# Two heads' scores in row halves of the array, one exponential over two banks, and a new order of work

## What is computed

```
x = x + L0_attn_ref(layernorm(x), ...)   # one head of width 64, causal softmax
x = x + L0_ffn_ref(layernorm(x), ...)    # one product in fp8
x = x + L1_attn_ref(layernorm(x), ...)   # 16 heads of width 16, rotary, causal softmax
x = x + L1_ffn_ref(layernorm(x), ...)    # sigmoid(r) * (relu(k)^2 @ W_v)
...
scores = jnp.einsum('bhsd,bhtd->bhst', Q, K) / jnp.sqrt(jnp.float32(D_K))
scores = jnp.where(causal[None, None], scores, -jnp.inf)
attn = jax.nn.softmax(scores, axis=-1)
out = jnp.einsum('bhst,bhtd->bhsd', attn, V)
```

## Time and profile before

| | |
|---|---|
| runs | 3010.06 us median of 3 (3002.6 to 3011.0) |
| the profiled execution | 3001.34 us, its span 2999.5 us |
| PE busy | 2646.3 us, 88% |
| DVE busy | 2010.0 us, 67% |
| ACT busy | 1566.6 us, 52% |
| POOL busy | 392.3 us, 13% |
| mean granted clock of PE | 0.946 of 2.4 GHz |

### The profile page before, as it was taken

The page is one execution under the profiler, slowest core; times in us unless marked ns, Lnnn a source line. Parts: engine busy times, 40 slices in busy tenths (PEclk is TensorE's granted clock), DMA queues, the critical chain, the costliest instruction groups (busy, mean ns, idle before and its releaser), DMA issues.

```text
span 2999.5 us, 49751 instructions
## 1 busy us (share of the span) xinstructions
PE 2646.3 (88%) x17886; PEld 1164.8 (39%) x18098; DVE 2010.0 (67%) x4386; ACT 1566.6 (52%) x3137; POOL 392.3 (13%) x418
## 2 busy tenths in 40 slices
PE   3677879999899898989989898998989989999995
PEld 2343423433343343434334343443434334433344
DVE  4445577776776767777665777777567577777832
ACT  1223336565555545565554555656454565666761
POOL 2212201010201111020100202020110100000011
PEclk8788879999999999999999999999999999999997
DMA  2333113030311313030120313122131121111101
GB/s 53 90 98 84 34 57 104 18 105 15 89 53 35 96 43 93 29 107 22 49 85 29 86 47 95 35 65 69 30 98 34 34 85 56 44 46 35 31 24 37
DMA packets 239478, 175.56 MB, mean 59 GB/s; under 512 B 89793, under 2 KB 238978, under 8 KB 239234
## 3 DMA queue, kind: packets, MB, share of 16 engines
q1 hardware_dynamic: 237376, 170.52, 20.1%
q10 hardware_dynamic: 1858, 1.84, 0.2%
HBM read 87.30 MB, written 84.41 MB: 57 GB/s over the span
## 4 chain that ended last, share of the span: by engine, by line
PE 69%; DVE 10%; ACT 6%; SPq 5%; issue 4%; DMA 3%; DVEq 1%; POOL 1%; another core or an unknown queue 1%; POOLq 0%; ACTq 0%
PE psum L1480 15%; PE psum L1466 14%; PE psum L1441 9%; DVE mx L1208 6%; SPq L719 4%; PE psum L1377 4%; PE psum L1409 4%; ACT probs L1010 3%; PE psum L1299 3%; DMA rest_dram<-parts 2%; PE psum L1508 2%; PE psum L1351 2%; PE psum L1527 2%; PE psum L1515 2%; PE psum L1428 2%
## 5 line engine op out<-in xcount | busy, mean ns | idle before, releaser
L1208 DVE TENSOR_REDUCE mx<-psum 128x1 f32<-128x512 f32 (+3 forms) x2560 | 1389.2, 600 | 409.1 <-PE psum L1447 229.2
L1010 ACT ACTIVATE probs<-psum 128x512 f32<-128x512 f32 (+3 forms) x2560 | 1186.7, 542 | 639.6 <-PE psum L1466 282.3
L1466 PE MATMUL psum<-qst,kst 98*128 98x512 bf16 (+7 forms) x2348 | 670.6, 357 | 84.5 <-ACT probs L1010 48.6
L1480 PE MATMUL psum<-probs,vs 128*17 128x512 f32 (+3 forms) x5120 | 600.0, 541 | 1.8 <-ACT probs L1010 0.4
L1441 PE MATMUL psum<-kst,qst 64*128 64x512 bf16 (+3 forms) x2560 | 450.9, 364 | 83.7 <-ACT probs L1010 33.8
L1466 PEld LDWEIGHTS psum<-qst,kst 98*128 98x128 bf16 (+1 forms) x2560 | 226.9, 99 | 505.0 <-ACT probs L1010 200.6
L1441 PEld LDWEIGHTS psum<-kst,qst 64*128 64x128 bf16 x2560 | 124.1, 94 | 541.3 <-DVE mx L1208 190.5
L1469 PE MATMUL psum<-maskf,identb 128*128 128x128 bf16 x1024 | 208.2, 225 | 4.1 <-issue 2.8
L856 POOL TENSOR_SCALAR vare<-mv 128x4 f32<-128x4 f32 x64 | 14.6, 228 | 1384.2 <-DVE mv L1106 1384.2
L970 ACT ACTIVATE probs<-psum 128x1024 f32<-128x1024 f32 x80 | 74.5, 938 | 150.0 <-PE psum L1357 100.7
L1447 PE MATMUL psum<-maskq,identh 64*128 64x128 bf16 x2048 | 151.3, 224 | 0.0
(11 more groups left out here) (133 smaller groups left out, 2548.8 us busy)
## 6 DMA issues: line engine op xcount, KB each, us to landing
main_dram<-parts SPq DMA_DIRECT2D x256, 128.0 KB
rest_dram<-parts SPq DMA_DIRECT2D x128, 128.0 KB
qst<-main_dram SPq DMA_DIRECT2D x128, 128.0 KB, 2.7
kst<-main_dram SPq DMA_DIRECT2D x128, 128.0 KB, 2.7
v_dram<-vst SPq DMA_DIRECT2D x64, 136.0 KB, 4.5
vs<-v_dram SPq DMA_DIRECT2D x64, 136.0 KB, 2.3
xs<-x_in SPq DMA_DIRECT2D x16, 512.0 KB, 4.0
x_dram<-xs SPq DMA_DIRECT2D x16, 512.0 KB, 2.9
```

Source lines behind the costliest of these rows:

```text
L1010: act.activation(probs[:, HG * (step_no(b, hg, k) % 2) + h, 0:cols], home("scores", item)[:, 0:cols], ACT.Exp, scale=DK1 ** -0.5).then_inc ...
L1208: dve.tensor_reduce(mx1[:, n % 2, 2 * g + odd, i % TPC, c:c + 1], bank(PLAN.home["max", item[:5]][odd], 0, width(i, c)), AX.X, ALU.max).th ...
L1466: ins = pe.matmul(ps[:, 0:CH - off], kst[rows, kslot, odd, g, P * (kb % TPC):P * (kb % TPC + 1)], qst[rows, qslot, odd, g, off:CH], start= ...
L1480: ins = pe.matmul(bank(7, off, CH, rows=VW, row=32 * h), vtile[:, h, :], probs[:, HG * (step_no(b, hg, k) % 2) + h, 0:CH - off], start=(kb ...
```

## The change

**Scores.** A `scores` job is now a pair of heads. The stacks `kst` and `qst` are laid out so that each head of the pair has its own 64 partitions: part 0 holds its MAIN rows (64), part 1 its REST rows and the two rows of the maximum (34 rows). The job is four matmuls, two side by side for each part, and four small ones for the mask. It takes an aligned pair of banks, one bank per head, and counts as R. `maskf` is gone.

**Exponential.** One instruction reads both banks, 2 x 512, where two instructions read 512 each. FAR_S goes from 4 heads to 2 pairs.

**Start.** The three memsets of `kst` and `qst` on DVE are gone; POOL sets the part-1 half of `kst` to ones, behind its first `root` job.

**Order.** The planner now assumes 0.31 us for leaving F and 0.1 or 0.14 us for the other switches (0.1 us for any before), STICK is 100 instead of 10, LEAD 85 instead of 66, and V0's assumed duration 1.85 instead of 0.9. The `max` jobs' banks are still E.

```
-LEAD = 66.0
+LEAD = 85.0
...
-STICK = 10.0
+SWITCH = {("F", "R"): 0.31, ("F", "C"): 0.31, ("R", "F"): 0.1, ("R", "C"): 0.1, ("C", "F"): 0.14, ("C", "R"): 0.14}
+STICK = 100.0
...
-FAR_M, FAR_S = 2, 4
+FAR_M, FAR_S = 2, 2
...
-                    time += 0.1
+                    time += SWITCH.get((mode, md), 0.0)
...
-    add("PE", "V0", c, key(), 0.9, *both(0), lat=0.1, claim="P", mode="F")
+    add("PE", "V0", c, key(), 1.85, *both(0), lat=0.1, claim="P", mode="F")
...
-                add("PE", "scores", (b, hg, k, h), key + h / 2, 0.215 * size + (0.055 if diagonal else 0),
-                    ("rows", me), ("load k", (b, hg, kb // TPC)), ("exp", far), lat=0.1, claim="P", mode="F")
-                add("ACT", "exp", (b, hg, k, h), key + h / 2, 0.05 + 0.427 * size, ("scores", (b, hg, k, h)),
+                add("PE", "scores", (b, hg, k, pair), key + pair, 0.43 * size + (0.11 if diagonal else 0),
+                    ("rows", me), ("load k", (b, hg, kb // TPC)), ("exp", far), lat=0.1, claim="D", mode="R")
+                add("ACT", "exp", (b, hg, k, pair), key + pair, 0.07 + 0.853 * size, ("scores", (b, hg, k, pair)),
...
+                    if item == (0, 0, 0):
+                        pool.memset(kst[:, :, 1, :, :], 1.0).then_inc(done, 1)
...
-                    act.activation(probs[:, HG * (step_no(b, hg, k) % 2) + h, 0:cols], home("scores", item)[:, 0:cols],
-                                   ACT.Exp, scale=DK1 ** -0.5).then_inc(S["exp"], 1)
+                    at = HG * (step_no(b, hg, k) % 2) + 2 * pair
+                    act.activation(probs[:, at:at + 2, 0:cols], two_banks("scores", item)[:, :, 0:cols], ACT.Exp,
+                                   scale=DK1 ** -0.5).then_inc(S["exp"], 1)
...
-            dve.memset(kst[HALF + REST:P, :, 0, :, :], 1.0).then_inc(S["stacks"], 1)
-            dve.memset(kst[REST:HALF, :, 1, :, :], 1.0).then_inc(S["stacks"], 1)
-            dve.memset(qst[REST:HALF, :, 1, :, :], 0.0).then_inc(S["stacks"], 1)
...
-                    g, odd = divmod(h, 2)
-                    rows = slice(0, P if odd else HALF + RROWS)
...
-                    ins = pe.matmul(ps[:, 0:CH - off], kst[rows, kslot, odd, g, P * (kb % TPC):P * (kb % TPC + 1)],
-                                    qst[rows, qslot, odd, g, off:CH], start=True, stop=not diagonal)
+                    for part in range(2):
+                        for odd in range(2):
+                            rows = slice(HALF * odd, HALF * odd + (HALF if part == 0 else RROWS))
+                            ins = pe.matmul(two[odd][:, 0:CH - off], kst[rows, kslot, part, pair, keys],
+                                            qst[rows, qslot, part, pair, off:CH],
+                                            start=(part == 0), stop=(part == 1 and not diagonal))
...
```

More of the change, by code:

```diff
@@ L343, in head_jobs @@
         add("SP", "load k", me, pos - LEAD - 25, 0.4, ("put", (b, q, 2 + hg // 2)),
-            *[("scores", n and (*n, h)) for h in range(HG)], lat=4.5)
+            *[("scores", n and (*n, pair)) for pair in range(HG // 2)], lat=4.5)
         slot = block_before(b, hg, q, QRING)
@@ L377, in head_jobs @@
             two = step_before(b, hg, k, 2)
[L378 to L379 removed]
+            for pair in range(HG // 2):
+                scored.append((b, hg, k, pair))
                 far = scored[-1 - FAR_S] if len(scored) > FAR_S else None
[L381 to L385 removed]
+                add("PE", "scores", (b, hg, k, pair), key + pair, 0.43 * size + (0.11 if diagonal else 0),
+                    ("rows", me), ("load k", (b, hg, kb // TPC)), ("exp", far), lat=0.1, claim="D", mode="R")
+                add("ACT", "exp", (b, hg, k, pair), key + pair, 0.07 + 0.853 * size, ("scores", (b, hg, k, pair)),
+                    ("values", two), lat=0.1, free=("scores", (b, hg, k, pair)))
+            add("PE", "values", (b, hg, k), key + 5, 0.84 * size, ("exp", (b, hg, k, 0)), ("exp", (b, hg, k, 1)),
                 ("load v", (b, hg, kb // TPC)), ("values", (b, hg, k - 1) if kb else None), lat=0.1, claim="V" if kb == 0 else None, mode="C")
@@ L483, in freed @@
     if kind == "max":
-        return "max d", (*item, PLAN.home[name].index(n))
+        return FREED_BY[kind], (*item, PLAN.home[name].index(n))
     if kind == "WO0":
@@ L610, in build @@
         v_dram = nc.dram_tensor("v_dram", [B, NHG, P, NT, HG * VW], F32, kind="Internal").ap()
-        names = KINDS + ["weights", "weights later", "const", "stacks", "ready", "ready later", "chain d", "chain p", "apart"]
+        names = KINDS + ["weights", "weights later", "const", "ready", "ready later", "chain d", "chain p", "apart"]
         names += [f"load x {i}" for i in range(2)] + [f"store x2 {i}" for i in range(2)]
@@ L742, in _ @@
                     if old:
-                        for h in range(HG):
-                            wt.job("scores", (*old[:2], k, h))
+                        wt.job("scores", (*old[:2], k, 0))
+                        wt.job("scores", (*old[:2], k, 1))
                     loaded = S[f"{kind} {slot}"]
@@ L828, in _ @@
                                base=0, pattern=[[-1, P]], channel_multiplier=1).then_inc(done, 1)
[L829 to L831 removed]
+            n += 1
             wt.wait_ge("const", n)
@@ L1005, in _ @@
                 elif kind == "exp":
-                    b, hg, k, h = item
+                    b, hg, k, pair = item
                     wt.job("values", step_before(b, hg, k, 2))
@@ L1440, in _ @@
                         rows = slice(HALF * odd, HALF * (odd + 1))
-                        ins = pe.matmul(two[odd][:, 0:cols], qst[rows, qslot, odd, g, P * (i % TPC):P * (i % TPC + 1)],
-                                        kst[rows, kslot, odd, g, 0:cols], start=True, stop=c < q)
+                        ins = pe.matmul(two[odd][:, 0:cols], qst[rows, qslot, 0, g, P * (i % TPC):P * (i % TPC + 1)],
+                                        kst[rows, kslot, 0, g, 0:cols], start=True, stop=c < q)
                     if c == q:
@@ L1461, in _ @@
                     off = span(q, kb)
-                    ps = home(kind, item)
-                    g, odd = divmod(h, 2)
-                    rows = slice(0, P if odd else HALF + RROWS)
+                    two = [bank(n) for n in PLAN.home[kind, item]]
+                    keys = slice(P * (kb % TPC), P * (kb % TPC + 1))
                     diagonal = kb >= TPC * q
-                    ins = pe.matmul(ps[:, 0:CH - off], kst[rows, kslot, odd, g, P * (kb % TPC):P * (kb % TPC + 1)],
-                                    qst[rows, qslot, odd, g, off:CH], start=True, stop=not diagonal)
-                    if diagonal:
-                        ins = pe.matmul(ps[:, 0:P], identb[:, :], maskf[:, :], start=False, stop=True)
+                    for part in range(2):
[4 more added lines that the diff above has]
+                                            start=(part == 0), stop=(part == 1 and not diagonal))
+                    if diagonal:
+                        for part in range(2):
+                            for odd in range(2):
+                                rows = slice(HALF * odd, HALF * (odd + 1))
+                                ins = pe.matmul(two[odd][:, 0:P], identh[rows, part, :], maskk[rows, part, :],
+                                                start=False, stop=(part == 1))
                     ins.then_inc(S["scores"], 1)
@@ L1473, in _ @@
                     q, kb = STEPS[k]
-                    for h in range(HG):
-                        wt.job("exp", (b, hg, k, h))
+                    wt.job("exp", (b, hg, k, 0))
+                    wt.job("exp", (b, hg, k, 1))
                     v_loaded(wt, b, hg, kb // TPC)
```

28 lines of the change are left out of this document (9 added, 19 removed).

## The result

| | before | after |
|---|---|---|
| median of the runs | 3008.60 us (3002.6 to 3011.0, 4 runs) | 3109.69 us (3103.1 to 3111.4, 4 runs) |
| ratio | | 1.0335, 95% interval 1.0312 to 1.0358 |
| span of the profiled run, granted clock | 2999.5 us, 0.946 | 3109.4 us, 0.953 |

The change costs 3.4%, or 101 us. The forecast was 3062: right in direction, inside its range of 2960 to 3130, and 48 us short. After is where the forecast's own range (3019 to 3110) and that of the rival that puts every wait on top (3110 to 3150) meet.

A forecast was written before the change was run, and what follows sets the result against it. PE was taken to bound the kernel, with 508 us of its span lost to waits and lower clock. 2999.5 - 75.5 - 5 + 120 + 21 = 3060, with 1.8 us around the span 3062 us; range 2960 to 3130.

The forecast's parts named there:

- Scores in halves: PE's scores: two slots of two matmuls side by side take 0.44 us a pair as before; price 0, 13 us either way.
- Changes of use: PE switching between kinds of matmul: 2594 fall to 1799, at 0.095 us each, 75.5 us less.
- that way of being wrong: Sign against the forecast: a change out of F in fact costs 0.31 us, giving 132 us more gain.
- One exponential per pair: ACT: the double form takes 1.02 us, four single ones 2.06, so ACT's work changes by 0 us.
- Banks: Scores wait on PE for banks held by the double exponential: +120 us in light steps, +21 in other blocks.
- the count's 201.9: Us of waits counted in PE's new order, at 377 places where scores reuse the home of the scores just before.
- The sign of 3.1 us for a light step: Steps in blocks with PE work under 3.0 us a step would take near 3.1 us if the forecast was right.
- Start: Without DVE's three memsets the first layernorm and all behind it come 5.1 us earlier: -5 us; POOL's fill costs 0.
- Waits in lost time: Faster rival: bank waits on PE replace time lost anyway, 2919 us at best, 2995 at most, middle 2965; chance 0.22.
- cancelling: Rival: 78 to 95 us of new waits on PE cancel the gains, within 0.3% of no change; chance 0.08.
- The clock: Rival: short waits bring PE's light steps to a granted clock of 0.88, +110 us, so 3170; chance 0.07.
- Everything on top: Slower rival: the whole 202 us of bank waits on PE is new, and more, 3110 to 3150 us; chance 0.13.

The follow-up runs named there:

- e5: After with any two banks for a pair of scores, an exponential per head, and before's LEAD, STICK and switch prices: 3010.9 us, 1.0019 of before.
- e11: Before with only STICK raised from 10 to 100: 3110.45 us, 1.0343 of before.
- e3: After planned with the old numbers (LEAD 66, STICK 10, 0.1 us per change of use, V0 0.9): 3137.19 us, 1.0426 of before.
- e6: As e5, but the two heads of scores take neighbouring banks in three aligned homes, each still with its own exponential: 3159.6 us, 1.0515 of before.
- e2: After with max pairs planned on an aligned pair of banks instead of any two: 3122.04 us, 1.0372 of before.
- e9: After with double exponential kept, scores in any two neighbouring banks (six places instead of three), before's LEAD, STICK and switch prices: 3106.5 us, 1.0324 of before.
- e12: e5 with LEAD 58 instead of 66, STICK 20 instead of 10, and the early fill of e8: 3031.36 us, 1.0083 of before.
- e4: Before, with single heads, planned with the new numbers (LEAD 85, STICK 100, dearer changes of use, V0 1.85): 3113.79 us, 1.0348 of before.
- e7: After in the same order, each exponential reading only the left half of its two banks' columns, probabilities zeroed first: 3047.41 us, 1.0135 of before.
- e10: e5 with STICK 15 instead of 10, scores up to three places ahead instead of two, and the early fill of e8: 3027.73 us, 1.0060 of before.
- e1: After with separate banks: scores pairs only in homes 0-1 and 2-3, max pairs in any two of banks 4 to 6: 3240.13 us, 1.0768 of before.
- e8: After with GpSimd's fill of the key tiles' second half issued right behind the constants: 3098.71 us in one run.

## Why the prediction was right or wrong

**The terms.** Three of them can be measured in the two traces; the waits are then what is left of the 110 us by which the span grew. The time at half clock is read from the records of the granted clock: 324 us before and 294 after, in which PE is busy for 196 and 212 us. Half of that, 98 and 106, is my estimate of what the lower clock cost.

| term | forecast | measured |
|---|---|---|
| changes of use, 2594 to 1799 | -75.5 | -75.5 (0.09 to 0.11 each between neighbouring starts, in every direction) |
| start | -5 | -1.3 |
| time at the lower clock | 0 | 98 to 106, +8 (less by up to 5, as before lacks records of matmuls) |
| waits of PE, with the rest (halves, keys) | +120 +21, 0 +-25 | +179, by difference |
| sum | +60.5 | +110 |

**Scores in halves: right.** A pair takes 0.44 (1442.91 to 1443.35 above), and e5, which has them, is within 0.3% of before.

**Changes of use: right.** For example `values` to `max` 0.99 (1441.70 to 1442.69), `max` to scores 0.22 without a change. The 0.31 of the planner is the price of a change in no distance, so that way of being wrong did not occur. But the term stood alone in my sum, and the numbers that bring it have a price of their own: e11 saves 37 us of changes and is 100 us slower.

**One exponential per pair: right on the path, with a size off.** ACT by form in after:

```profile
L1009 ACT ACTIVATE probs<-psum 128x1024 f32<-128x1024 f32 x896 | 898.0, 1023 | 621.0 <-PE psum L1464 513.1 <-PE psum L1471 90.6 <-PE psum L1483 17.1
```

1023 ns as read from the first layer. ACT's busy time fell from 1566.6 to 1505.8 us, not by 0; how much of it the span saw is open (e3 is 0.9% below e6, with another V0 and another order).

**Banks: right mechanism, and this is the term that was mis-sized.** "let the new wait swallow half of the 0.2 of short ones" and "of the 43 us in the other blocks I take half" took 61 us off the count's 201.9. The traces show about 20 off: 179 us by the table came on top, 38 more than the 141 that I took. In the light steps 0.36 us was new where the forecast had 0.32, 135 us in all against 120; the other 44, where it had 21, came outside them. With 4 us less at the start and up to 8 from the clock, that is the gap of 49 us between the spans. (The sign of 3.1 us for a light step did not follow from the forecast's own terms: 2.42 + 0.49 + 0.32 = 3.23, and 3.27 was measured.)

That the count came so near is partly luck, though. It looked only at scores behind the scores just before them. It missed three things: scores wait in ScalarE's queue (the second pair's exponential follows the first's), a bank may be held by an older job, and maxima wait for VectorE in the same way. Within one form it ranked e2 and e3 correctly; between forms it failed: by its waits alone it said 42 us for e6 over e5 (149 measured) and 97 for e9 under e3 (31). Mended for these after e5 to e11, as told in the expectation of e12, it gives, in us above before:

| | after | e2 | e3 | e4 | e5 | e6 | e7 | e9 | e10 | e11 | e12 | e1 |
|---|---|---|---|---|---|---|---|---|---|---|---|---|
| waits counted, less before's 135 | 197 | 189 | 198 | 142 | 98 | 207 | 136 | 131 | 119 | 112 | 79 | 114 |
| changes of use x 0.095 | -76 | -69 | -63 | -45 | -61 | -62 | -76 | -63 | -72 | -37 | -64 | -53 |
| sum | 121 | 120 | 135 | 97 | 37 | 146 | 61 | 68 | 47 | 75 | 14 | 61 |
| measured | 101 | 112 | 128 | 104 | 7 | 156 | 43 | 96 | 18 | 100 | 23 | 230 |

Eleven of twelve are within 30 us. Of the 197 us of after, it puts 119 on scores behind exponentials (54 to 173) and 70 on maxima behind VectorE (44 to 114). PE's own idle time in the traces has 69 and 50 us more of the two (above). The 5 us of the early fill in e10 and e12 are not in the table. e1 it misses by 169 us. The larger part of that is the clock, which the count does not have: e1 is at half clock for 713 us, and PE is busy for 431 of them where before it is for 196; half of the difference is 118 us. The rest is open. Differences of 20 us are below what the count can tell (e12). It is a count fitted to the runs; what the runs alone show is e7 (holding time), e6 (three homes) and e11 (STICK, and waits for maxima). How much of the 101 us of after falls to the homes, to the double exponential and to the new numbers is not shown: the runs change them one at a time only on other orders.

**Start: wrong.** The first layernorm is early by more than the 5.1 us forecast (its statistics begin at 20.50, before at 26.69), but I set POOL's `kst` fill against the second `root` only. It took 5.22 us instead of the 6.2 forecast, runs beside VectorE's first TENSOR_SCALAR and holds it up for about its own length: PE's first transpose comes at 30.19 instead of 31.50, 1.3 us earlier, where e8, without the fill there, has 25.30.

**The rivals.** Waits in lost time, and cancelling: both fell, as some 180 of the 202 us were new. The clock: not in after (0.953); it is real in e1 (0.890), e4, e11 and e12, though. "Everything on top" had a chance of 0.13, and its mechanism is the nearest to what came, at the very edge of its range; I had put it low because 0.49 us were lost in a light step anyway, and the runs show that this lost time took in only 0.06 of the 0.42.

## What to carry to other kernels

A wait added between neighbouring jobs on the engine that bounds the kernel adds to its old waits unless the trace shows the old wait at that very place; an average loss per step is no measure of what it will cover (here 0.49 us covered some 0.06 of 0.42). When an instruction reads two buffers at once, count before adopting it how often their next user comes sooner than the pair is released, in each reader's queue and for every kind of user, and measure the same edit with a free choice of place. A number that saves changes of use by keeping like jobs together has to be judged by what it does to the engine that reads their results, and to the granted clock.

## What the runs showed that I had not expected

VectorE can be held up by a fill on GpSimd. In after one TENSOR_SCALAR of 128x256 took 5286 ns where the three others took about 400, and it ended within 0.2 us of GpSimd's 5.22 us MEMSET, which had started 0.08 us earlier (23.71 and 23.79). In e7 a second fill follows the first, and the group of four takes 9.70 us. The instruction in after (shortest, median and longest in ns):

```profile
L1116 DVE TENSOR_SCALAR xn<-xs,mv,rstd x4: 394/400/5286, 23.8 to 29.6; 128x256 f32<-128x256 f32 x4
```

and of e7 on the timeline:

```profile
23.58 5.22 POOL L856 MEMSET kst<- 128x6144 bf16 x1
28.74 3.51 POOL L857 MEMSET probs<- 128x4096 f32 x1
...
23.66 9.70 DVE L1118 TENSOR_SCALAR xn<-xs,mv,rstd 128x256 f32<-128x256 f32 x4 [1.48 <-POOL rstd L854]
```

In e8, with no fill beside it, it is 1.38. The Trainium skill, "SBUF — State Buffer", Who interferes with whom, has this rule: VectorE and GpSimd share a pair of ports under an exclusive lock, `tensor_scalar` can use it if its operands allow, and whoever issues first keeps it for the whole instruction while the other blocks. The traces agree: GpSimd was first by 0.08 us, and VectorE stood for the whole fill.

The granted clock depends on the order, not on the amount of work: 0.946 before, 0.924 with one number of the order changed (e11), and 0.890 with after's work and other banks (e1) where after has 0.953. What in the order does it, no run here separates.
